# An adaptive-norm mixture-of-experts kernel: x and the rows of h turned in squares by VectorE, scale and shift of x on ScalarE, full low products in the router, and a beginning without GpSimd

## What is computed

```
x1     = (64 * x + sum over the batch's tokens of x) * q      # per batch and feature
h      = relu(x1 @ W2 + b2)                                   # [8192, 512]
logits = h @ gate_w.T                                         # 64 experts
scores = softmax(logits); the 6 best experts per token, each expert keeps its first 64 tokens
y      = sum over kept (token, expert) of score * ((silu(h @ wg[e]) * (h @ wu[e])) @ wd[e])
shared = (silu(h @ sw_gate) * (h @ sw_up)) @ sw_down          # inner width 704
out    = x + y + shared
```

## Time and profile before

| | |
|---|---|
| median of 3 runs | 1317.76 us |
| the profiled execution | 1318.17 us, of which the span from first to last instruction is 1316.3 |
| PE (TensorE) busy | 1291.7 us, 98% of the span |
| VectorE (DVE) | 663.3 us, 50% |
| ScalarE (ACT) | 370.2 us, 28% |
| GpSimd (POOL) | 169.2 us, 13% |
| DMA, mean | 191 GB/s |

### The profile page before, as it was taken

One profiled execution on the slowest core, in us unless ns is written; L12 is line 12 of the kernel. 1 busy time (PEld: TensorE's weight loads), 2 busy tenths in 40 slices (PEclk: granted clock), 3 DMA queues, 4 the chain that ended last, 5 costly groups with the idle time before them and its releaser, 6 DMA issues.

```text
span 1316.3 us, 16591 instructions
## 1 busy us (share of the span) xinstructions
PE 1291.7 (98%) x6424; PEld 962.8 (73%) x6424; DVE 663.3 (50%) x1430; ACT 370.2 (28%) x611; POOL 169.2 (13%) x129
## 2 busy tenths in 40 slices
PE   4899999999999999999999999999999999999999
PEld 3688888888888888888876666666666667666666
DVE  6685785857758577684742323223232232323322
ACT  2734443343433434334322112111121111211111
POOL 2400000000000000000001222222222222222220
PEclk7999999999999999999999999999999999999999
DMA  6434305142150522503666897997989889798952
GB/s 199 166 111 141 123 37 174 55 172 93 53 194 18 176 89 76 188 5 140 230 209 216 256 320 243 307 317 221 317 291 282 285 268 333 233 298 281 292 138 76
DMA packets 97006, 250.94 MB, mean 191 GB/s; under 512 B 17632, under 2 KB 17760, under 8 KB 94752
## 3 DMA queue, kind: packets, MB, share of 16 engines
q1 hardware_dynamic: 85440, 224.70, 47.9%
q0 software_dynamic: 11488, 25.17, 9.5%
HBM read 197.14 MB, written 61.10 MB: 196 GB/s over the span
## 4 chain that ended last, share of the span: by engine, by line
PE 97%; DVE 1%; ACT 1%; DMA 0%; issue 0%; SPq 0%; ACTq 0%; DVEq 0%
PE bank L1107 23%; PE bank L1109 22%; PE bank L1108 22%; PE bank L1331 12%; PE bank L1354 7%; PE bank L1141 2%; PE bank L1117 2%; PE bank L1313 1%; PE bank L1215 1%; PE bank L1214 1%; PE bank L1165 1%; PE bank L1154 1%; PE bank L1155 1%; PE bank L1340 1%; DVE xm L800 0%; DMA w3s<-in_L_cond_W_dram 0%
## 5 line engine op out<-in xcount | busy, mean ns | idle before, releaser
L1107 PE MATMUL bank<-hh,gu 128*128 128x512 f32 x704 | 281.3, 400 | 0.0
L1109 PE MATMUL bank<-hh,gu 128*128 128x512 f32 x704 | 274.6, 390 | 0.0
L1108 PE MATMUL bank<-hl,gu 128*128 128x512 f32 x704 | 274.3, 390 | 0.0
L1107 PEld LDWEIGHTS bank<-hh,gu 128*128 128x128 f32 x704 | 132.5, 188 | 38.0 <-issue 12.8
L817 DVE TENSOR_TENSOR prod<-bank,prod 128x512 f32<-128x512 f32 x96 | 66.3, 690 | 176.8 <-PE bank L1109 156.5
L1109 PEld LDWEIGHTS bank<-hh,gu 128*128 128x128 f32 x704 | 132.1, 188 | 28.6
L1108 PEld LDWEIGHTS bank<-hl,gu 128*128 128x128 f32 x704 | 132.4, 188 | 25.3
L578 ACT ACTIVATE ah<-prod 128x512 fp32r<-128x512 f32 x96 | 60.6, 632 | 262.0 <-DVE prod L817 262.0
L1107 PE MATMUL bank<-sdh,ah 128*128 128x512 f32 x320 | 128.2, 401 | 0.0
L1109 PE MATMUL bank<-sdh,al 128*128 128x512 f32 x320 | 124.9, 390 | 0.0
L1108 PE MATMUL bank<-sdl,ah 128*128 128x512 f32 x320 | 124.8, 390 | 0.0
(11 more groups left out here) (123 smaller groups left out, 1705.8 us busy)
## 6 DMA issues: line engine op xcount, KB each, us to landing
wg<-in_L_ffn_w_gate_dram SPq DMA_DIRECT2D x64, 704.0 KB, 9.2
wu<-in_L_ffn_w_up_dram SPq DMA_DIRECT2D x64, 704.0 KB, 11.2
wd<-in_L_ffn_w_down_dram SPq DMA_DIRECT2D x64, 512.0 KB, 5.3
x<-in_x_dram SPq DMA_DIRECT2D x16, 1024.0 KB, 8.7
table<-hrow SPq DMA_DIRECT2D x16, 1024.0 KB, 4.4
wd<-in_L_ffn_w_down_dram SPq DMA_DIRECT2D x64, 192.0 KB, 6.1
out_dram<-outst SPq DMA_DIRECT2D x36, 256.0 KB, 3.4
hT<-h SPq DMA_DIRECT2D x8, 1024.0 KB, 3.9
```

What stands on the lines that cost most here:

```text
L1107: nc.tensor.matmul(o, st_h, mv_h, start=first_mm, stop=False)
L1108: nc.tensor.matmul(o, st_h, mv_l, start=False, stop=False)
L1109: return nc.tensor.matmul(o, st_l, mv_h, start=False, stop=last_mm)
```

## The change

- **x** is loaded as 32 partitions per quarter of the features: four DMAs per chunk, 512 bytes at a time, so that a transpose in squares of 32x32 on VectorE (`turn_x`, in place) gives features on partitions. A partition then holds four features, 4p to 4p+3, side by side (k is the innermost index); W2, b2, b3, W3, gate_w, sw_gate and sw_up are read in the same order of features. All passes over the turned tile step by four elements.
- **Scale and shift**: VectorE makes only the sums and the products sum * q (`sum_shifts`). ScalarE makes 64q * x + shift, one operation per batch and k, 64 columns each, eight per 128 tokens (`shift_x`). For half of chunks 0 and 1 VectorE does it.
- **Rows of h** are turned by VectorE in squares (`take_rows`, called ahead of `split_h`) and stored by four DMAs in pieces of 512 bytes. PE no longer has `transpose_x` and `rows_tile`.
- **Router**: the low part of h is multiplied with all 128 columns; `logits` is four transposes, and `route` adds the two halves with a copy and an addition. logits_raw waits for each low part by itself and has its own bank; cond tiles rotate over three banks.
- **Beginning**: low parts of the weight pieces are made by VectorE; there are four staging buffers; chunk 0 is worked in half-width cond products; pieces 1 to 6 come later in every queue. `body(0)` has an order of its own on ScalarE and VectorE.
- **Order**: in body(i), x of chunks c+2 and d+2 is loaded behind store_out(i, 1), and turn_x(c+2, 0) stands between merge(i, 6) and take_down(v, 2).

```diff
+        def xm_made(n, j):
+
+            if n < 2:
+                by_vector = (j < 2) if n == 0 else (j >= 2)
+                return (s.xm_begun if by_vector else s.xm_ready), 2 * n + j % 2 + 1
+            return s.xm_ready, J * (n - 1) + j + 1
...
+                    for j in (1, 3):
+                        sp.wait_ge(*xm_made(n - 2, j))
+                load_x_half(n, 0, CH // SQ, x_loaded[n % 2])
+
+            def load_x_half(n, b0, b1, came):
+                for a in range(4):
+                    sp.dma_start(x32[a * SQ:(a + 1) * SQ, n % 2, b0:b1, :],
+                                 xf[n * CH + b0 * SQ:n * CH + b1 * SQ, a * P:(a + 1) * P].rearrange(
+                                     "(b i) c -> i b c", i=SQ)).then_inc(came, 16)
...
-                sp.dma_start(table[n * CH:(n + 1) * CH, 0:D].rearrange("(j p) r -> p j r", p=P),
-                             hrow[:, :, :]).then_inc(s.rows_stored, 16)
+                for a in range(4):
+                    sp.dma_start(table[n * CH:(n + 1) * CH, a * P:(a + 1) * P].rearrange("(b i) c -> i b c", i=SQ),
+                                 hrow[a * SQ:(a + 1) * SQ, :, :]).then_inc(s.rows_stored, 16)
...
                     store_out(i, 1)
+                    if i < ND - 2:
+                        load_x(c + 2)
+                        load_x(d + 2)
...
-            for n, (_, parts) in enumerate(pieces):
-                for k, (h_part, l_part, src) in enumerate(parts):
-                    pool.wait_ge(s.stage_split_h, splits_before[n] + k + 1)
-                    nc.gpsimd.tensor_tensor(l_part, src, h_part.bitcast(F32),
-                                            ALU.subtract).then_inc(s.stage_split_l, 1)
...
+            def shift_x(n, j, half):
+
+                if half == 0:
+                    act.wait_ge(s.shift_ready, J * n + j + 1)
+                    if n == 1:
+                        act.wait_ge(s.xml_ready, j + 1)
+                    elif n % 2 == 0:
+                        wait(act, s.xml_ready, J * (n - (1 if j < 2 else 0)) + j % 2 + 1 if n > 0 else 0)
+                    elif j < 2:
+                        act.wait_ge(s.xml_ready, J * (n - 1) + j + 3)
+                    else:
+                        act.wait_ge(s.al_ready, KT * (n // 2))
+                b = n * BPC + j * BPT + half
+                xt = x_tile(n, j).rearrange("p (b t k) -> p b k t", k=KC, b=BPT)
+                o = xm_place(n, j).rearrange("p (k b t) -> p b k t", k=KC, b=BPT)
+                for k in range(KC):
+                    op = nc.scalar.activation(o[:, half, k, :], xt[:, half, k, :], ACT.Identity,
+                                              bias=shift[:, n % 2, j, k, half:half + 1], scale=qnT[:, k, b:b + 1])
+                if half == BPT - 1:
+                    op.then_inc(s.xm_ready, 1)
...
-            def take_rows(n, oc):
-                if oc == 0:
-                    wait(act, s.rows_stored, 16 * n)
-                act.wait_ge(s.rows_filled, KC * n + oc + 1)
-                copy(hrow[:, :, oc * P:(oc + 1) * P],
-                     bank[7][:, :].rearrange("p (j f) -> p j f", j=J)).then_inc(s.rows_taken, 1)
...
                 take_cond(b, 0)
-                exp_scores(a)
+                if 0 < i < ND - 1:
+                    shift_x(c, 0, 0)
                 take_cond(b, 1)
-                take_rows(b, 0)
+                if i > 0:
+                    exp_scores(a)
+                if 0 < i < ND - 1:
+                    shift_x(c, 0, 1)
                 take_cond(b, 2)
-                take_rows(b, 1)
+                take_cond(b, 3)
                 if i == 0:
                     split_piece(5)
-                take_cond(b, 3)
-                take_rows(b, 2)
+                    split_piece(6)
+                    shift_x(c, 0, 0)
+                    shift_x(c, 0, 1)
+                if not more:
...
+                split_xm(c, 0)
+                shift_x(c, 1, 0)
+                take_lraw(b)
+                shift_x(c, 1, 1)
+                split_xm(c, 1)
+                silu(v, 0)
+                shift_x(c, 2, 0)
+                split_a(v, 0)
+                shift_x(c, 2, 1)
+                silu(v, 1)
                 if i == 0:
-                    split_piece(6)
-                take_rows(b, 3)
-                take_lraw(b)
-                if more:
-                    split_xm(c, 0)
-                silu(v, 0)
-                if more:
-                    split_xm(c, 1)
-                split_a(v, 0)
-                silu(v, 1)
-                if more:
-                    split_xm(c, 2)
-                else:
-                    exp_scores(b)
+                    exp_scores(a)
+                split_xm(c, 2)
+                shift_x(c, 3, 0)
                 split_a(v, 1)
-                if more:
-                    split_xm(c, 3)
+                shift_x(c, 3, 1)
                 silu(v, 2)
+                split_xm(c, 3)
+                shift_x(d, 0, 0)
...
+            def turn_x(n, j):
+
+                for q in (j, j + 1):
+                    if n == 0 and q == 0:
+                        dve.wait_ge(x_begun, 64)
+                    elif q == (2 if n == 0 else 0):
+                        dve.wait_ge(x_loaded[n % 2], 64 * (n // 2 + 1))
+                    t = x_tile(n, q).rearrange("p (b j k) -> p b k j", k=KC, j=SQ)
+                    nc.vector.transpose(t, t).then_inc(s.x_turned, 1)
+                for q in (j, j + 1):
+                    dve.wait_ge(s.x_turned, J * n + q + 1)
+                    nc.vector.reduce_sum(vsum[:, q, :, :],
+                                         x_tile(n, q).rearrange("p (b t k) -> p k b t", k=KC, b=BPT),
+                                         AX).then_inc(s.vsum_step, 1)
...
+                for q in (j, j + 1):
+                    dve.wait_ge(s.vsum_step, J * n + q + 1)
+                    nc.vector.tensor_tensor(shift[:, n % 2, q, :, :], vsum[:, q, :, :], of_batches(qT, n, q),
+                                            ALU.mult).then_inc(s.shift_ready, 1)
...
+            def take_rows(n, oc):
+
+                dve.wait_ge(s.cond_taken, KC * n + oc + 1)
+                if oc == 0:
+                    wait(dve, s.rows_stored, 64 * n)
+                nc.vector.transpose(hrow[:, :, oc:P:KC],
+                                    h32[:, oc, :].rearrange("p (b i) -> p b i", i=SQ)).then_inc(s.rows_taken, 1)
+
+            def split_piece(n):
+                for k, (h_part, l_part, src) in enumerate(pieces[n][1]):
+                    dve.wait_ge(s.stage_split_h, splits_before[n] + k + 1)
+                    lower(l_part, src, h_part).then_inc(s.stage_split_l, 1)
...
+                link(nc.vector.tensor_copy(lg[:, :, :], parts[:, 1, :, :]))
+                link(nc.vector.tensor_tensor(lg[:, :, :], parts[:, 0, :, :], lg[:, :, :], ALU.add))
...
+                if i == 0:
+                    for k in range(KC):
+                        split_h(b, k)
+                        if k < 2:
+                            split_piece(3 + k)
+                    turn_x(c, 0)
+                    sum_shifts(c, 0)
+                    split_piece(5)
+                    split_piece(6)
+                else:
+                    split_h(b, 0)
+                    route(a)
+                    split_h(b, 1)
+                    split_h(b, 2)
+                    score(a)
+                    split_h(b, 3)
                 if i > 0:
-                    merge(i - 1, 5)
-                split_h(b, 3)
-                if i > 0:
-                    merge(i - 1, 6)
                     take_down(v - 1, 3)
...
                 product(v, 0)
-                split_xm(c, 1)
-                split_a(v, 0)
-                take_xt(c, 2)
-                product(v, 1)
-                split_xm(c, 2)
-                split_a(v, 1)
-                split_xm(c, 3)
+                if i == 0:
+                    route(a)
+                    split_a(v, 0)
+                    product(v, 1)
+                    score(a)
+                    split_xm(c, 2)
+                    split_a(v, 1)
+                    split_xm(c, 3)
+                    route(b)
+                    turn_x(d, 0)
+                    sum_shifts(d, 0)
+                else:
+                    route(b)
+                    split_a(v, 0)
+                    product(v, 1)
+                    split_xm(c, 2)
+                    turn_x(d, 0)
+                    sum_shifts(d, 0)
+                    split_a(v, 1)
+                    split_xm(c, 3)
                 product(v, 2)
...
+                turn_x(d, 2)
+                sum_shifts(d, 2)
                 split_a(v, 4)
                 product(v, 5)
-                take_xt(d, 0)
                 split_a(v, 5)
+                split_h(c, 0)
+                merge(i, 3)
+                split_h(c, 1)
                 score(b)
-                split_h(c, 0)
-                split_h(c, 1)
-                take_xt(d, 2)
                 split_h(c, 2)
```

(65 more changed lines are left out.)

328 lines of the change are left out of this document (152 added, 176 removed).

## The result

The changed kernel takes **1335.82 us** (median of 4 runs, 1333.74 to 1337.07), beside 1317.72 for the kernel before on the same chip: ratio 1.0136, 95% interval 1.0124 to 1.0149. It is slower by 18.1 us; the forecast was 1272, faster. The profiled execution took 1333.74 us (span 1332.0), 15.6 more than the one of before.

What follows compares the result with a forecast made beforehand. PE was taken to bound the kernel from chunk 2 on. From 1318.17 us, 51.8 less PE work and 6.5 at the beginning came off and 12.3 of stalls were added: 1272 us, range 1257 to 1297.

Steps and rivals of the forecast that it cites:

- The work taken from PE: After chunk 2 starts, PE loses transposes of x and h (46.2 us) and logits work (5.6): 51.8 us gained.
- The logits: On PE, each logits call falls from 0.84 to 0.44 us as four transposes; 14 calls save 5.6 us.
- the new wait: VectorE's turn_x waits for x of the next pair, loaded behind store_out; PE stalls in logits_raw, bodies 0 to 5.
- L: Time from take_down done until the next pair's x lands: 7.75 us, bounds 6.45 and 11.
- I take 0.61: VectorE's price in us for a transpose in squares, taken equal to any 512-column operation.
- transpose group over 1 us: Sign of a wrong forecast: VectorE's transpose groups, expected at 0.6 to 0.7 us, taking over 1 us.
- the strided rival: Four-element steps make VectorE's passes half dearer (0.9 us), 2.4 more per pair: 1290; doubled, about 1308; chance 0.25 for both.
- the beginning, 6.5 us of gain: Before chunk 2: first product near 20 us, gate-up near 55, chunk 2 at 93.5 instead of 99.99; bounds 0 and 11.
- The stall: PE waits in logits_raw for the last low part of h from VectorE: 2.05 us in six bodies, 12.3 lost.
- the cover of 5.7 us: L up to 5.7 us is hidden by PE's own work; each further us stalls PE in six bodies.
- the forecast's own formula for the stall: PE's stall per pair is L beyond 5.7 us plus any growth of VectorE's chain behind x, in six bodies.
- Scale-and-shift: ScalarE's 64 operations of 64 columns per pair: 0.30 us each, bounds 0.20 and 0.41, 19 us in all.

Runs made afterwards that it cites:

- experiment 1: Changed kernel with the load of x for chunk c+2 issued earlier on SP, ahead of the second scores store: 1276.17 us, ratio 0.9685.
- experiment 3: Changed kernel with x loaded early and all passes over x and rows of h contiguous (features mixed up): 1262.25 us, ratio 0.9583.
- the square of experiments 1 to 3: Four kernels: changed 1335.82 us; with x loaded early 1276.17; with contiguous passes, features mixed up, 1301.16; with both 1262.25.
- experiments 5 and 6: Changed kernel with one DMA in 2 KB pieces instead of four, per load of x: 1327.02 us; per chunk's rows of h: 1321.15 us.
- experiment 9: Kernel with x loaded early, body(0) reordered on ScalarE and VectorE (silu and product ahead of preparing chunk 3): 1272.84 us, ratio 0.9662.
- experiment 7: Changed kernel with exp_scores(a) and the second half of shift_x(c, 0) moved behind take_cond(b, 3) on ScalarE: 1341.84 us, ratio 1.0183.

## Why the prediction was wrong, by its steps

**Held.** The work taken from PE: forecast 51.8 us after chunk 2; experiment 1 shows 1216.3 - 1165.2 = 51.1, with a pair of 72.15 against 72.7. That the two totals are so near is in part luck: the removed work was a little dearer (8.3 us a pair instead of 7.8; experiment 3 gains 54.5), and experiment 1 still loses about 3 us of it in the pair behind the beginning. The logits were sized right. The place of the new wait was right as well, and its cause (x of the next pair behind store_out on SP) and the six bodies in which it falls.

**Failed: L, "SP issues store_out at once, 0.43 plus a gap".** The forecast had load_x start 0.55 us after the down tile, at 462.4; it was 465.40, 3.0 later. Four stores of rows and the landing of store_out(i, 0), which load_xr(i, 2) waits for, stood in front; I had walked VectorE's and PE's queues there and not SP's. From the first issue to landing it took 8.8 us instead of 7.2: the fourth issue stands 1.86 behind the first, which the working had not counted. L was 12.4 where the sum had 7.75 and its upper bound 11. The changed kernel itself, the square of experiments 1 to 3 and experiments 5 and 6 show it.

**Failed: "I take 0.61".** Read start to start, as the forecast was: the pair of transposes at 474.24 is followed by the reduction at 476.20, so 0.98 each, and hrow to hl is 0.93. The group stands at 1102 ns, the "transpose group over 1 us" that the forecast had named as a sign of being wrong. VectorE's chain from turn_x to the last hl took 16.7 us (474.24 to 490.97) instead of 14.3, the 2.4 that the strided rival had named. That rival was right on the mechanism, and I had put it at 0.25 with "what slows a weight load need not slow VectorE". The Trainium skill (SBUF — State Buffer, the note on cachelines in Door 1) had it: an access that crosses to a new 16-byte line pays. By that rule the traces agree on VectorE (1.09 or 1.04 against 0.69 or 0.66) and on ScalarE (3.87 against 1.91 us for W2), and TensorE's weight load in the earlier trace rows was a fair sign.

**Failed: the beginning, 6.5 us of gain.** It was 9.4 of loss. The first product came at 24.7 (forecast 20.2), gate-up at 63.8 (55), and from there to chunk 2 it took 45.6 us (38.5). The steps explain 11.8 of the 15.9 (experiment 3 against 1): W2's low part alone took 3.8 where the working had 2.2. The rest, 98.1 against 93.5, lies ahead of gate-up: without steps that starts at 59.3 (forecast 55), and from there to chunk 2 it takes 38.8, as forecast. What holds that first part up was not tested. By experiment 9 another order brings chunk 2 forward by 12.7 us, but only 2.1 of them are left at the end while the passes have steps. Whether more would be left with contiguous passes was not run.

**The stall.** Forecast 2.05 us, measured 9.6 in the mean of six. For the pair shown: 4.6 from L, 2.4 from the passes, and a rest of about 0.9, which I put down to products at the 1.2 GHz level, make the 2.05 into 10 (8.2 of wait and 1.85 more for the eight router products). Which engine lets PE go was wrong too (hh on ScalarE, not hl on VectorE), but experiment 7 shows both nearly equally late: with ScalarE's part moved, the waits of the six pairs fall from 44.6 to 39.7 us, 0.8 a pair. Beyond the cover of 5.7 us nothing is hidden, and each us counts six times: that is why L, 1.4 above its bound, and passes at the price of the strided rival left the range together.

**With the sizes measured** the forecast's sum is 1318.17 - 51.1 + 9.4 + 57.4 = 1333.9, and the profiled execution took 1333.74. These three sizes are differences between the same runs, so the sum has to close; it shows how the loss is shared out, and proves nothing. With the forecast's own formula for the stall (9.1 a pair, below) in place of 57.4 it gives 1331. Scale-and-shift was sized low as well (four start within 1.66 us, about 0.39 apart, for 0.30, inside the bounds); with ScalarE at 51 in 72.15 it cost nothing in a steady pair.

**The range** had 1297 as its upper end. It took the strided case as a rival and the late x as a bound of L, one at a time, each with the other at its likeliest value. They share a chain, so the case in which both hold had to be priced; with L = 12.4 and 2.4 more of passes the forecast's own formula gives a stall of 12.4 - 5.7 + 2.4 = 9.1, so 55 us in six bodies, more than the 51.8 gained, before the beginning is counted.

## What to carry to other kernels

Before a load is put behind other entries of a DMA queue, walk that queue as one walks an engine's: each issue has its price, and an entry that waits for a buffer holds all that stand behind it. Where two unsure costs lie on one chain that has some cover, price them together; the first uses the cover up and the second counts in full. A layout that makes one transfer handy but leaves every pass over the tile with steps of 16 bytes is paid in each pass: put the steps where there are fewest passes (no kernel here tries this).

## What was new of the hardware

- A pass of 128x512 fp32 in steps of four elements takes 1.04 to 1.10 us on VectorE, contiguous 0.66 to 0.71; the transpose in squares (0.69 to 0.71) is no dearer than a copy (0.69). On ScalarE the dense pass over W2 (2048 columns) doubles, 3.87 against 1.91, the 64-column one goes from 428 to 488 ns.
- DMA issues in pieces of 512 bytes: four stores of rows hold SP for 4.20 us and eight loads of x for 7.48, where the same rows in one DMA with pieces of 2 KB hold it for 0.37. Issues and pieces were changed together.
- Behind one unbroken wait of 6.7 to 8.2 us, PE's granted clock was at 0.50 for 3.4 to 4.4 us of work; where about the same wait was cut in pieces, it was at 0.50 for 10.2 to 13.5 us, these waits included (six stalls each).
- While GpSimd made subtractions of two SBUF inputs, three of four of VectorE's took 2.9 to 3.4 us instead of 0.67 for 128x512, and its transposes, with one input, stayed at 1.09.
